# Feed-forward gates and ups as three float32r products in a one-core transformer kernel

## The reference, cut to what matters

```python
def ffn_layer(x, g, bln, W1, b1, W2, b2):
    mu = x.mean(-1, keepdims=True)
    var = ((x - mu) ** 2).mean(-1, keepdims=True)
    xn = (x - mu) / jnp.sqrt(var + 1e-05) * g + bln
    hg = xn @ W1 + b1
    a, gate = jnp.split(hg, 2, -1)
    return a * jax.nn.gelu(gate, approximate=False) @ W2 + b2
for i in range(DEPTH):        # 6
    x = attn_layer(shift_tokens(x), Wqkv[i], q_scale[i], k_scale[i], Wo[i]) + x
    x = ffn_layer(shift_tokens(x), ln_g[i], ln_b[i], W1[i], b1[i], W2[i], b2[i]) + x
```

## Time and profile before

| | |
|---|---|
| median of 3 runs | 2494.8 us (2491.49 to 2495.09) |
| the profiled execution | 2506.73 us, its span 2504.8 us |
| busy in the span | PE 2354.9, DVE 1717.0, ACT 1597.2, POOL 1451.3 us |
| transformer layers | from about 200 to about 1850 us of the span |
| mean granted TensorE clock | 0.966 of 2.4 GHz |

### The profile page before, as it was taken

One profiled execution on the slowest core, in us unless ns is written; L12 is line 12 of the kernel. 1 busy time (PEld: TensorE's weight loads), 2 busy tenths in 40 slices (PEclk: granted clock), 3 DMA queues, 4 the chain that ended last, 5 costly groups with the idle time before them and its releaser, 6 DMA issues.

```text
span 2504.8 us, 121652 instructions
## 1 busy us (share of the span) xinstructions
PE 2354.9 (94%) x53677; PEld 1748.5 (70%) x53677; DVE 1717.0 (69%) x3393; ACT 1597.2 (64%) x5036; POOL 1451.3 (58%) x1408
## 2 busy tenths in 40 slices
PE   9958999999999999999999999999888999999967
PEld 8836777777777777677777777777645666666657
DVE  4477788777888888787788788887335555555534
ACT  3226777777777787777777778777625454545422
POOL 1166667656676676566666677665117656656307
PEclk9969999999999999999999999999979999999978
DMA  4013333433333334333343333333216222222136
GB/s 91 15 33 86 79 83 94 97 80 83 91 93 95 82 83 103 83 92 87 80 96 90 80 92 87 87 87 87 54 30 177 49 48 48 48 48 48 31 97 249
DMA packets 230208, 204.60 MB, mean 82 GB/s; under 512 B 133687, under 2 KB 155464, under 8 KB 229552
## 3 DMA queue, kind: packets, MB, share of 16 engines
q1 hardware_dynamic: 225296, 190.91, 30.5%
q0 software_dynamic: 2208, 5.58, 0.7%
q10 hardware_dynamic: 2176, 0.33, 0.1%
HBM read 86.05 MB, written 15.70 MB: 41 GB/s over the span
## 4 chain that ended last, share of the span: by engine, by line
PE 66%; DVE 12%; SPq 6%; ACT 5%; issue 5%; POOL 4%; DMA 3%; POOLq 0%; ACTq 0%; DVEq 0%
PE psum L1211 7%; PE psum L1959 5%; PE psum L1237 5%; PE psum L1229 5%; PE psum L1938 4%; PE psum L1111 4%; PE psum L1944 3%; PE psum L1113 3%; PE psum L1112 3%; PE psum L1993 3%; PE psum L1983 3%; ACT p L1357 3%; SPq L972 3%; PE psum L1188 2%; PE psum L1219 2%
## 5 line engine op out<-in xcount | busy, mean ns | idle before, releaser
L1357 ACT ACTIVATE p<-p,stat 128x64 f32<-128x64 f32 x1536 | 512.4, 336 | 47.2 <-DVE stat L1491 44.9
L1577 POOL TENSOR_TENSOR p<-p,inverse 128x512 f32<-128x512 f32 x192 | 200.2, 1043 | 456.5 <-DVE inverse L1494 452.2
L1211 PE MATMUL psum<-kT,qT 32*32 32x64 f32 x24576 | 305.5, 224 | 25.8 <-issue 24.2
L2092 DVE TENSOR_REDUCE largest<-psum 128x1 f32<-128x512 f32 x256 | 165.0, 687 | 228.0 <-PE psum L1944 228.0
L1211 PEld LDWEIGHTS psum<-kT,qT 32*32 32x32 f32 x24576 | 264.1, 103 | 75.3 <-issue 74.3
L1357 ACT ACTIVATION_READ_ACCUMULATOR p<-p,stat 128x1 f32 x1536 | 288.6, 188 | 0.0
L1421 DVE SCALAR_TENSOR_TENSOR rotated<-psum,scales,rotary 128x512 f32<-128x512 f32 x384 | 270.8, 742 | 25.8 <-ACT sq L1293 25.8
L1556 POOL TENSOR_TENSOR squares<-sq 128x512 f32<-128x512 f32 x192 | 245.3, 1278 | 44.3 <-ACT sq L1293 43.8
L1293 ACT ACTIVATE sq<-psum 128x512 f32<-128x512 f32 x384 | 213.7, 582 | 57.3 <-PE psum L1113 54.6
L1229 PEld LDWEIGHTS psum<-pT,v_win 64*64 64x64 f32 x12288 | 198.6, 136 | 64.7 <-issue 45.9
L1111 PE MATMUL psum<-xs,wqkv_high 128*128 128x512 f32 x384 | 205.7, 536 | 23.2 <-DVE rotated L1421 22.9
(11 more groups left out here) (351 smaller groups left out, 5402.3 us busy)
## 6 DMA issues: line engine op xcount, KB each, us to landing
v_win<-v_tok SPq DMA_DIRECT2D x576, 128.0 KB
rnorm_wide<-rnorms SPq DMA_DIRECT2D x384, 64.0 KB
v_win<-v_tok SPq DMA_DIRECT2D x336, 64.0 KB
q_rows<-q_rows_all SPq DMA_DIRECT2D x32, 512.0 KB, 4.6
tile_weights<-expert_table SPq DMA_DIRECT2D x23, 512.0 KB, 5.8
wqkv<-L_ffn_Wqkv SPq DMA_DIRECT2D x96, 64.0 KB, 2.2
rel_values<-sq SPq DMA_DIRECT2D x60, 64.0 KB, 2.2
wo<-L_ffn_Wo SPq DMA_DIRECT2D x48, 64.0 KB
```

Source lines behind the costliest of these rows:

```text
L1211: last = PE.e.matmul(psum[WIN * blk:WIN * (blk + 1), f, out], q[rows, g, half, tok:tok + WIN], k[rows, g, half, tok:tok + 2 * WIN], start= ...
L1357: last = A.e.activation(p, p, ACT.Exp, bias=t.stat[:, h, 2 * g + f:2 * g + f + 1], accum_out=t.sum[:, h, g, f:f + 1])
L1577: G.e.tensor_tensor(p, p, t.inv[:, h, :, :].unsqueeze(3).to_broadcast([P, GROUPS_TF, 2, 2 * WIN]), ALU.mult).then_inc(*t.p_scaled.by(m))
L2092: V.e.tensor_reduce(t.mx[n % 4][:, :], psum[:, n % 5, :], AX, ALU.max, negate=True).then_inc(*t.largest.by(n))
```

## The change

It makes each gate and each up three float32r matmuls in place of one float32 matmul. For that the normalised input `xc` is split for each unit at step 90 (ACT `xn_high`, POOL `xn_low`), and W1 for each layer at step 84 of its first unit (ACT `w1_high`, POOL `w1_low`, from a landing place inside `t.act`, loaded at step 79 rather than with W2). The first gate moves from step 91 to 94. To make room, three things lose a spare buffer: `pT` (one for two), `norms` (one for two), and the squares (three in a ring for four, POOL adds in place). The third chunk has 85 columns and is filled with zero columns to 128.

```diff
-FFN_AT = {..., "spread": 88, "scale": 89, "gate0": 91, "gate1": 95, "gate2": 96, "gelu": 99,
+FFN_AT = {..., "spread": 88, "scale": 89, "split": 90, "gate0": 94, "gate1": 95, "gate2": 96, "gelu": 99,
           "up0": 100, "up1": 101, "up2": 104, "down": 108, "add": 109}
+UP_AT = {"load": 79, "split": 84}
+def squares_at(u, p, half=0):
+    return (2 * GROUPS_TF * u + p + half) % 3
...
+def load_up(c, t, u):
+    SP, l = c.SP, u // B
+    if u:
+        SP.wait_ge(*t.f_down.on(u - 1))
...
+    SP.e.dma_start(t.w1_raw, c.io["L0_ffn_W1"][l]).then_inc(*t.w1_in.by(l))
...
         if s == FFN_AT[f"gate{j}"]:
-            PE.wait_ge(*t.f_normed.on(u))
-            PE.wait_ge(*t.w_in.on((l, 3)))
+            PE.wait_ge(*t.f_low.on(u))
+            PE.wait_ge(*t.w1_low.on(l))
             ps = ring_take(c, t, "unit", u, f"gate{j}")
-            PE.e.matmul(ps[0:n, :], t.w1[:, DI + lo:DI + lo + n], t.xc[:, :], start=True, stop=True).then_inc(*t.f_gates.by((u, j)))
+            three_products(PE, ps, [w[:, DI + lo:DI + lo + P] for w in t.w1], x).then_inc(*t.f_gates.by((u, j)))
         if s == FFN_AT[f"up{j}"]:
             ps = ring_take(c, t, "unit", u, f"up{j}")
-            PE.e.matmul(ps[0:n, :], t.w1[:, lo:lo + n], t.xc[:, :], start=True, stop=True).then_inc(*t.f_up.by((u, j)))
+            three_products(PE, ps, [w[:, lo:lo + P] for w in t.w1], x).then_inc(*t.f_up.by((u, j)))
...
+            if half and p % 2 == 0 and (u or p):
+                A.wait_ge(*t.summed.on((u, p - 1) if p else (u - 1, 2 * GROUPS_TF - 1)))
...
+    if s == FFN_AT["split"]:
+        A.wait_ge(*t.f_normed.on(u))
+        if u:
+            A.wait_ge(*t.f_up.on((u - 1, 2)))
+        A.e.activation(t.xn[0][:, :], t.xc[:, :], ACT.Copy).then_inc(*t.f_high.by(u))
+    if s == UP_AT["split"] and b == 0:
+        A.wait_ge(*t.w1_in.on(l))
...
+        A.e.activation(t.w1[0][:, 0:2 * DI], t.w1_raw, ACT.Copy).then_inc(*t.w1_high.by(l))
...
-        if m >= 2:
-            A.wait_ge(*t.weighted.on(m - 2))
+        if m:
+            A.wait_ge(*t.weighted.on(m - 1))
...
+    if s == FFN_AT["split"]:
+        G.wait_ge(*t.f_high.on(u))
+        G.e.tensor_tensor(t.xn[1][:, :], t.xc[:, :], t.xn[0][:, :].bitcast(F32), ALU.subtract).then_inc(*t.f_low.by(u))
+    if s == UP_AT["split"] and b == 0:
+        G.wait_ge(*t.w1_high.on(l))
+        G.e.tensor_tensor(t.w1[1][:, 0:2 * DI], t.w1_raw, t.w1[0][:, 0:2 * DI].bitcast(F32), ALU.subtract).then_inc(*t.w1_low.by(l))
```

More of the change, by code:

```diff
@@ L721 @@
 HALF_AT = (0, 1)
-FFN_AT = {"shift": 80, "center": 83, "square": 84, "sum": 84, "root": 84, "spread": 88, "scale": 89, "gate0": 91, "gate1": 95, "gate2": 96, "gelu": 99,
+FFN_AT = {"shift": 80, "center": 83, "square": 84, "sum": 84, "root": 84, "spread": 88, "scale": 89, "split": 90, "gate0": 94, "gate1": 95, "gate2": 96, "gelu": 99,
           "up0": 100, "up1": 101, "up2": 104, "down": 108, "add": 109}
@@ L791, in transformer_setup @@
     t.xf = sb("x_ffn", [P, S])
+    t.w1 = [sb(n, [P, W1_COLUMNS], F32R) for n in ("w1_high", "w1_low")]
+    t.xn = [sb(n, [P, S], F32R) for n in ("xn_high", "xn_low")]
+    t.w1_raw = t.act[:, 0:2, :].rearrange("p a s -> p (a s)")[:, 0:2 * DI]
     t.q = [sb(f"qT{i}", [P, GROUPS_TF, 2, S]) for i in range(2)]
@@ L795, in transformer_setup @@
     t.wide = [sb(f"rnorm_wide{i}", [P, S]) for i in range(2)]
-    t.norms, t.rn, t.rn_t = [sb(f"norms{i}", [P, P]) for i in range(2)], [sb(f"rnorm{i}", [P, P]) for i in range(2)], t.wide[0][:, 0:P]
+    t.norms, t.rn, t.rn_t = [sb("norms", [P, P])] * 2, [sb(f"rnorm{i}", [P, P]) for i in range(2)], t.wide[0][:, 0:P]
     t.rn_dram = [nc.dram_tensor(f"rnorms{i}", (32, S), F32, kind="Internal").ap() for i in range(2)]
@@ L828, in transformer_setup @@
     t.shift_high, t.shift_low = per("shift_high", units, halves), per("shift_low", units, halves)
+    t.w1_in = Signal(nc, "tf_w1_in", layers, 16)
+    t.w1_high, t.w1_low, t.f_high, t.f_low = one("w1_high", layers), one("w1_low", layers), one("ffn_high", units), one("ffn_low", units)
     t.tab_turned, t.tab_kept = one("tables_turned", TABLES), one("tables_kept", TABLES)
@@ L936, in transformer_sync @@
                         load_projections(c, t, then, after)
+            if s == UP_AT["load"] and b == 0:
+                load_up(c, t, u)
             if s == NORM_AT["out"]:
@@ L1141, in unit_tensor @@
             for k in range(TPB):
-                last = PE.e.matmul(ps[32 * k:32 * k + 32, 0:P], t.onehot[:, kind * GROUPS_TF + g, :], t.sq_both[x % 2][:, k * P:(k + 1) * P], start=(x < p), stop=(x == p))
+                last = PE.e.matmul(ps[32 * k:32 * k + 32, 0:P], t.onehot[:, kind * GROUPS_TF + g, :], t.sq[squares_at(u, x)][:, k * P:(k + 1) * P], start=(x < p), stop=(x == p))
         last.then_inc(*t.summed.by((u, p)))
@@ L1229, in part_tensor @@
                         last = PE.e.matmul(psum[to:to + DH, 2 + o, at:at + WIN], v[rows, blk, 2 * (2 * a + o) + h, :],
[L1230 removed]
+                                           t.pt[rows, 2 * a + o, blk * WIN:(blk + 1) * WIN], start=True, stop=True)
         last.then_inc(*t.weighted.by(m))
@@ L1518, in transformer_pool @@
         G.e.memset(low[:, :].bitcast(F32), 0.0)
+    for w in t.w1:
+        G.e.memset(w[:, 2 * DI:].bitcast(F32), 0.0)
     for k in t.k:
@@ L1552, in unit_gpsimd @@
         G.wait_ge(*t.squared.on((u, (p, 1))))
-        if u or p >= 2:
-            before = p - 1 - p % 2
-            G.wait_ge(*t.summed.on((u, before) if before > 0 else (u - 1, 2 * GROUPS_TF - 1)))
-        G.e.tensor_tensor(t.sq_both[p % 2][:, :], t.sq[0][:, :], t.sq[1][:, :], ALU.add).then_inc(*t.squares.by((u, p)))
+        x, y = (t.sq[squares_at(u, p, half)][:, :] for half in range(2))
+        G.e.tensor_tensor(x, x, y, ALU.add).then_inc(*t.squares.by((u, p)))
     p, at = divmod(s - MADE_LAG, 4)
```

28 lines of the change are left out of this document (17 added, 11 removed).

## The result

The change made the kernel slower. The changed kernel takes 2506.11 us (median of 8, 2500.56 to 2510.22), the kernel before, run on the same chip, 2494.04 us (median of 8, 2488.25 to 2499.17); the ratio is 1.0051, 95% interval 1.0036 to 1.0066. That is 12 us slower, outside my range of 2473 to 2499, and on the side to which I gave 0.12.

The account below looks back on a forecast made before the run. It took PE, busy 97% in the layers, to bound the kernel. Terms -11.4 + 0.5 + 4 - 1 + 0.7 = -7.2 took the profiled 2506.73 to 2499.5; less the 12 us to the median, 2487.5 us, range 2473 to 2499.

Parts of the forecast that it names:

- PE's own work sets most of the time: In the layers PE is busy 97% at full clock, so taking PE work away was to shorten the time.
- my 21.6 us: PE's saving on six gate and up products a unit: 0.15 us each, 0.90 a unit, over 24 units.
- 11.4: Part of PE's saving expected to show after waits at the second gate for the v_tok copy: -11.4 us.
- Where it counts: PE reaches the second gate 0.15 earlier: First gate leaves its place ahead of the mix (-0.85), comes behind the round-29 projection (+0.70); second gate then waits for v_tok.
- units that gain 0.90 each: The 9 units whose window chain is shorter than PE's way to the second gate: -9 x 0.90.
- For W1's 682 columns ... zero, bounded by their own sum, 6 x 2.6 = 16: Splitting W1 on ACT and POOL, six times at round 20 where POOL waits for DVE: 0, at most 16 us.
- Rival D: DVE and POOL hinder each other; added subtractions delay scalings and lengthen the window chain: slower, 2504 us; chance 0.12.
- The split of the input, +0.5 and +4: Mixes waiting for oT behind ACT's new copy, +0.5 us; POOL's added subtraction delaying the turn, +4 us.
- Buffers, norms, squares: nothing: Single pT, single norms and the squares' new wait cost nothing, since earlier program order covers them.
- The carried difference: Before's median lay 12 us under its profiled execution of 2506.73; the same 12 was taken off the forecast 2499.5.

Follow-up runs that it names:

- one, three and four products: Float32r products per gate and up, changed from the changed kernel without input split, first gate at step 91 (three products): 1.0055, 1.0024 and 1.0051 to before.
- the second column: Kernel before with only the buffers reduced (one pT, one norms, squares in a ring of three): 1.0003 to before; its profiled execution, 2497.24 us, gives the stretch times.
- mixed version: Changed kernel with the first gate left as one float32 matmul at step 91 and POOL's W1 subtraction cut into eight pieces: 1.0050 to before.

## Why the prediction was wrong

**The premise: "PE's own work sets most of the time".** This step failed. Busy 97% was read rightly but concluded from wrongly. The gates and ups save what I said: PE's busy time fell by 16.0 us. Of my 21.6 us, though, 4 us show with the gate at its old place (1.0041 to 1.0024, within the noise of the difference) and 9.5 with it moved (1.0089 to 1.0051). I had let 11.4 stand, so this term was too large by 2 to 7. The point is the slope: one, three and four products take 1.0055, 1.0024 and 1.0051. PE's idle time before was short and spread, and another chain is about as long as PE's where PE was to gain. In stretch 8 this can be watched. The saving of stretches 6 and 7 (0.63, or 0.45 against the second column) brings PE early to a mix whose `oT` ACT copies behind its exponentials and squares, and 0.28 is lost at once; with one product of three the loss there is 1.31.

**"Where it counts: PE reaches the second gate 0.15 earlier".** The moved gate was booked as part of a gain. By itself it costs 7 us (1.0028). I had seen that the second gate would wait for `v_tok` (5.4 us more in the trace; I said 10), and with it +0.70 for the gate behind the release, but I set against that units that gain 0.90 each, and left the clock out. In the kernel with the gate moved alone, waits for `v_tok` of 14.0 us and up to 6.9 us of slower clock stand against the 7 us lost. In the changed kernel the clock is a small part, at most 1.7 us, though behind the wait of 1.33 us it cost 1.0.

**"For W1's 682 columns ... zero, bounded by their own sum, 6 x 2.6 = 16".** Mis-sized, and the largest single term of the error: it measured 0.0041 - 0.0003 = 0.0038, 9.5 us. The cover that I named, POOL waiting for DVE, was the wrong way round: POOL had the time, but its instruction stopped DVE for 1.42 us in each layer. Rival D had the mechanism, DVE and POOL hindering each other, and its time, 2504, was nearest. It had the place wrong: the key scaling has a mean of 1.77 us after, 1.75 before, and ACT's wait for the windows went only from 20.6 to 23.7 in the same stretch (21.5 in the earlier trace rows reaches to 1737 us; there it is 25.3 after). And it named only half of the hindering: POOL got 56.7 us busier in the stretch, not the 43 of rival D for the whole kernel, since its own products of the queries took longer, 1446 and 1767 ns for 1286 and 1647 (lines 1606 and 1607).

**The split of the input, +0.5 and +4.** The waits came, even more of them: `oT` 11.6 us, and the turn 8.3 for 3.8. But leaving the split out brought nothing back (1.0057 for 1.0051): the waits for `v_tok` and the slower clock grew instead. So these two terms can't be added to the others as I did.

**Buffers, norms, squares: nothing.** Right (1.0003).

**The carried difference.** I made the sum against the profiled execution and took 12 us off for the median. That of the changed kernel is 1.6 us below its median. One profile of this kernel is uncertain by as much as the effect in question.

My term of -11.4 us, products and moved gate together, measured +3 (-4 and +7), and W1's 0 measured +9.5; the +4.5 for the split and POOL's delay measured about 0. In ratios, buffers +0.03%, W1 +0.38%, moved gate +0.28%, products -0.17%, split of the input about 0 make +0.52%, and the change measured +0.51%. That they meet so closely is partly luck. Buffers, W1 and products are steps on the way to one kernel, so the sum is that kernel's 1.0024 and the moved gate's 1.0028, and it is uncertain by 0.0023. It also holds only with the products at the worth that they have at the old place of the gate; with -0.38% it would be +0.31%. The mixed version shows that such sums are no law here. What stays open is which chain takes over where PE gets shorter; the runs name three that are near (`v_tok` behind the windows, `oT` behind the exponentials, `p` behind DVE and POOL), and no run in which relief of one brought time back. No version beat the kernel before.

## What to carry to other kernels

A busy share of 97% does not make an engine the one that sets the pace. Take a part of its work away, or add some, and look at the slope before you pay for a saving with work on other engines.

An order tuned for short, spread waits is a resource. Moving one matmul, with no work added, cost 7 us of 2494, and the wait ahead of the second gate that it opened is what the trace shows of it. Where waits of over 1 us appear, add up the time at the lower clock too, before you blame it: it costs at most 1.7 us in the changed kernel, and up to 27 us where PE had one product of three.

Look for what a long POOL instruction meets on DVE, however small that is, not only for whether POOL has the time.

## What the runs showed of the hardware

- A wait of PE of 1.33 us within work at full clock came with a fall to the 1.2 GHz level, with matmuls of 512 columns 0.42 to 0.43 us apart in place of 0.23. Not every such wait did: of five between 1.14 and 1.53 us for `v_tok` in the changed kernel three did, and the longest did not. Taking 68 us of work from PE left it at a mean clock of 0.98 where it had 1.00, and the kernel got slower by 8 us.
- A DVE instruction on 128x4 elements took 1.58 us for 0.16 when POOL's subtraction of 682 columns had started 0.09 us before it.
- Cut into eight POOL subtractions of up to 86 columns, 0.372 us each, one split kept POOL busy for 2.65 us (15.9 for six), where one instruction of 682 columns took 1.65.
